# A routed first layer moved into token order, and a second stage that gathers its result

## The reference

```
xn  = layernorm(x)
# linear attention, 16 heads of 16
q, k = elu(xn@Wq+bq)+1, elu(xn@Wk+bk)+1 ; v = xn@Wv+bv
kv   = sum over the sequence of k (x) v, per head
att  = (q @ kv) / max(q . sum(k), 1e-6)  @ Wo + bo
# feed-forward: a shared expert and a routed one
swiglu(z) = silu(first half of z) * second half
shared = swiglu(xn @ w_in.T) @ w_out.T           # 256 -> 1024 -> 512 -> 256
group  = argmax(xn @ wg.T + gb)                  # 2 groups of 4 experts
p      = softmax(expert logits within the group) * group probability
h      = swiglu(xn @ w1.T)                       # the same w1 for all experts
routed = sum over the two best experts e of  p[e] * (h @ w2[e].T)
out    = x + att + shared + routed
```

## Time and profile before

| | |
|---|---|
| median of 3 runs | 1070.78 us (1067.65 to 1071.2) |
| profiled execution, own time | 1058.75 us |
| its span, first to last instruction | 1056.8 us |
| mean granted TensorE clock | 0.995 of full speed |
| busy: TensorE / weight loads | 1012.4 (96%) / 910.4 us (86%) |
| busy: VectorE / ScalarE / GpSimd | 672.9 (64%) / 398.8 (38%) / 491.5 us (47%) |
| DMA | 64.55 MB in 55585 packets, mean 61 GB/s |

### The profile page before, as it was taken

How to read it: one execution, slowest core, us unless ns; L and a number is a source line. 1 busy time by engine, 2 the same in 40 slices (tenths; PEclk the granted TensorE clock), 3 DMA queues, 4 the chain that set the end, 5 groups by cost and what they waited for, 6 DMA issues and landing times.

```text
span 1056.8 us, 21589 instructions
## 1 busy us (share of the span) xinstructions
PE 1012.4 (96%) x6662; PEld 910.4 (86%) x6663; DVE 672.9 (64%) x1681; ACT 398.8 (38%) x676; POOL 491.5 (47%) x489
## 2 busy tenths in 40 slices
PE   5999999999999999999999889999999999999996
PEld 5889879888888888898888779999999999999996
DVE  7887797788779778877977634444443444444343
ACT  3454354345445444544444322222222222222221
POOL 5343343534343443334344445555555555555534
PEclk9999999999999999999999899999999999999999
DMA  8012111201211120211111032222222122222321
GB/s 269 24 53 73 52 40 52 72 20 57 68 52 40 52 72 26 64 54 52 40 52 53 12 82 71 64 72 61 69 69 71 63 69 69 63 68 69 65 45 21
DMA packets 55585, 64.55 MB, mean 61 GB/s; under 512 B 18829, under 2 KB 45581, under 8 KB 55568
## 3 DMA queue, kind: packets, MB, share of 16 engines
q1 hardware_dynamic: 42624, 35.86, 11.3%
q0 software_dynamic: 12944, 28.47, 9.9%
HBM read 37.16 MB, written 28.58 MB: 62 GB/s over the span
## 4 chain that ended last, share of the span: by engine, by line
PE 60%; DVE 22%; issue 12%; ACT 3%; DMA 1%; POOL 1%; SPq 0%; DVEq 0%; ACTq 0%; POOLq 0%
PE bank L309 19%; PE bank L310 19%; PE bank L311 18%; DVE xn L715 4%; PE bank L381 3%; DVE stats L701 2%; DVE gated L795 1%; DVE lmax L726 1%; DVE phiq L825 1%; DVE phik L808 1%; PE bank L502 1%; ACT expt L617 1%; ACT expt L619 1%; ACT gated L598 1%; DVE rn L857 1%
## 5 line engine op out<-in xcount | busy, mean ns | idle before, releaser
L598 ACT ACTIVATE gated<-bank 128x512 f32<-128x512 f32 (+1 forms) x140 | 83.0, 593 | 264.2 <-PE bank L311 224.6
L309 PE MATMUL bank<-wexp_hi,h_hi 128*128 x600 | 170.2, 284 | 0.3 <-DVE h_lo L961 0.3
L310 PE MATMUL bank<-wexp_lo,h_hi 128*128 x600 | 168.5, 281 | 0.0
L311 PE MATMUL bank<-wexp_hi,h_lo 128*128 x600 | 168.5, 281 | 0.0
L997 POOL TENSOR_TENSOR h_lo<-gated,h_hi 128x512 fp32r<-128x512 f32 x64 | 83.8, 1309 | 170.5 <-ACT h_hi L602 169.0
L602 ACT CAST h_hi<-gated 128x512 fp32r<-128x512 f32 (+1 forms) x140 | 86.4, 617 | 159.1 <-DVE gated L795 158.4
L795 DVE TENSOR_TENSOR gated<-gated,bank 128x512 f32<-128x512 f32 (+1 forms) x140 | 95.2, 680 | 77.5 <-ACT gated L598 77.5
L971 DVE SCALAR_TENSOR_TENSOR res<-bank,cur,res 128x256 f32<-128x256 f32 x150 | 62.2, 477 | 123.1 <-PE bank L311 120.7
L1058 POOL DMA_INDIRECT out<-res,idx_cur x75 | 74.2, 989 | 102.9 <-DVE res L971 88.9
L309 PE MATMUL bank<-xnT_hi,wexp_hi 128*128 128x512 f32 (+1 forms) x304 | 117.7, 387 | 1.0 <-DVE xnT_lo L952 1.0
L310 PE MATMUL bank<-xnT_lo,wexp_hi 128*128 128x512 f32 (+1 forms) x304 | 117.7, 387 | 0.0
(11 more groups left out here) (171 smaller groups left out, 2506.6 us busy)
## 6 DMA issues: line engine op xcount, KB each, us to landing
xt<-x SPq DMA_DIRECT2D x16, 512.0 KB, 3.6
xn_d<-xn SPq DMA_DIRECT2D x16, 512.0 KB, 2.9
base_d<-res SPq DMA_DIRECT2D x16, 512.0 KB, 4.5
wstage<-w_exp SPq DMA_DIRECT2D x16, 320.0 KB, 4.2
tab_d<-wexp_hi SPq DMA_DIRECT2D x12, 128.0 KB, 5.5
phik<-tab_d SPq DMA_DIRECT2D x76, 2.0 KB
xn<-xn_d,idx_next POOLq DMA_INDIRECT x76, 2.8
res<-base_d,idx_cur POOLq DMA_INDIRECT x76
```

Source lines behind the costliest of these rows:

```text
L309: e.matmul(to, w_hi, m_hi_, start=first_, stop=False, skip_group_check=free)
L310: e.matmul(to, w_hi, m_lo_, start=False, stop=False, skip_group_check=free)
L311: return e.matmul(to, w_lo, m_hi_, start=False, stop=last_, skip_group_check=free)
L598: act.activation(gated[:, j % 2, 0:cols], bank[gate_bank][:, 0:cols], ACT.Silu).then_inc(sil, 1)
```

## The change

What moves:

- The routed first layer is computed in stage one, in token order: per tile 12 matmuls with the tile's xnT as weights and 512 columns of w1 moving (`routed(t, banks)`), a SiLU on ScalarE and a gate on VectorE into hs[t], a [128 tokens, 512] tile. hs lies in the buffers of phik and expt. w1's rows are permuted on the host in blocks of 32, and both halves of it are loaded and split before batch 0.
- GpSimd scatters, per batch and tile, the row of the table, the row of hs to `h_d` (2 KB) and the row of res to `base_d` (1 KB) to the token's place in its class: 12 indirect DMAs where there were 4. The stores of xn and of base by SyncE go; x is loaded a second time, into res, after the scatters of the batch before have landed.
- xn is made in place of x. VectorE makes ranks and table rows right after gate 1, ahead of the norm of the next batch, in every batch.
- The head sums have phiq moving and 32 columns of khead as weights, four tiles in the four column groups of bank 6; rn is [128, 128] (tile and head on the partitions), and `rdiag` puts each tile's block in its own 128 columns, so that one matmul of 512 columns per chunk spreads it. The transposes of rn go.
- After stage one SyncE writes zeros behind the end of each class in `h_d` and `base_d`: 13 times a position read and two stores.
- Stage two goes tile by tile, eight tiles per turn. SyncE loads the table piece and, in four DMAs of 32 partitions, the tile's h, 512 B per descriptor, so that VectorE's transpose of 32x32 blocks completes a transpose of 128x512. ScalarE makes the high part and issues the load of base; VectorE makes the low part and the two additions; TensorE has only the second layer, 24 matmuls of 256 columns.

The core of the diff (stage one, TensorE and VectorE):

```diff
+            def routed(t, banks):
+                for half in range(2):
+                    for c in range(DC):
+                        mm = mm3(pe, bank[banks[half]][:, :], xnT_hi[:, c, t * P:(t + 1) * P], xnT_lo[:, c, t * P:(t + 1) * P],
+                                 w1_hi[:, c, half * H1:(half + 1) * H1], w1_lo[:, c, half * H1:(half + 1) * H1], c == 0, c == DC - 1)
+                mm.then_inc(rh_done, 1)
...
-                for t in range(TB):
-                    for c in range(DC):
-                        mm = pe.matmul(bank[6][:, 16 * t:16 * t + 16], phiq[:, c, t * P:(t + 1) * P], khead[:, c, :],
+                for c in range(DC):
+                    for t in range(TB):
+                        mm = pe.matmul(bank[6][32 * t:32 * t + 32, 0:P], khead[:, c, :], phiq[:, c, t * P:(t + 1) * P],
...
+                routed(0, (0, 1))        # behind the transposes of kvm; then m, which waits for gate 2
+                hidden(3, (3, 7))
+                routed(1, (0, 1))
+                # spread; routed(2, (3, 7)); routed(3, (0, 1)); transposes(b + 1); y
...
                 gate(b, 1, 1)
+                ranks_in(b)
+                table_rows(b)
+                norm(b + 1)
                 gate(b, 2, 4)
+                dve.tensor_scalar(rn, bank[6][:, 0:P], EPS_N, None, ALU.max).then_inc(kstep, 1)
+                dve.reciprocal(rn, rn).then_inc(kstep, 1)
+                dve.tensor_copy(rhigh.bitcast(f32r), rn).then_inc(kstep, 1)
+                dve.scalar_tensor_tensor(rn, rhigh, low_row, rn, ALU.mult, ALU.add).then_inc(kstep, 1)
+                dve.tensor_tensor(rdiag, rn.unsqueeze(1).broadcast_to([P, TB, P]),
+                                  own_block.unsqueeze(2).broadcast_to([P, TB, P]), ALU.mult).then_inc(rn_rdy, 1)
+                routed_gate(b, 0, 1)
+                # m_lo, normalise(b + 1), gate 3, routed_gate 1, qn, qn_lo, routed_gate 2 and 3, t_low
```

GpSimd and SyncE in stage one:

```diff
+                pool.wait_ge(r_ld, 16 * (b + 1))
+                pool.tensor_tensor(res[:, :, :], res[:, :, :], bo..., ALU.add).then_inc(res_rdy, 1)
+                split(b + 2, b * UNIT + W1, UNIT)
+                low(0, ...); low(1, ...); reciprocal_root(b + 1)
+                for t in range(TB):
+                    scatter(tab_d, rows[:, t, :], t, row_st)
+                low(2, ...); scatter(h_d, hs[0], 0, hs_st); low(3, ...)
+                for t in range(1, TB):
+                    wait_apart(pool, rg_rdy, TB * b + t + 1)
+                    scatter(h_d, hs[t], t, hs_st)
+                for t in range(TB):
+                    wait_apart(pool, base_rdy, DC * b + t // 2 + 1)
+                    scatter(base_d, res[:, t, :], t, base_st)
...
+                    sp.wait_ge(t_done, DC * (b + 1))
+                    sp.dma_start(xt[:, :, :], x_rows(b + 1)).then_inc(x_ld, 16)
+                wait_apart(sp, base_st, 16 * TB * b)
+                sp.dma_start(res[:, :, :], x_rows(b)).then_inc(r_ld, 16)
+                sp.wait_ge(wexp_split, b + 2)
+                sp.dma_start(wstage[:, 0:UNIT], w_exp[:, bass.ds(b * UNIT + W1, UNIT)]).then_inc(w_ld, 16)
```

Stage two (SyncE, TensorE, ScalarE, VectorE):

```diff
+            def tiles_in(q):
+                wait_apart(sp, tab_ld, 16 * TB * q)
+                at = [sp.value_load(info_i[0:1, 2, bass.ds(q * TB + t, 1)], min_val=0, max_val=SENT) for t in range(TB)]
                 for t in range(TB):
+                    sp.dma_start(tab[:, bass.ds(q * TB + t, 1), :]..., tab_d[bass.ds(at[t], P), :]).then_inc(tab_ld, 16)
+                    wait_apart(sp, tr_done, TB * q + t - 3)
+                    for i in range(4):
+                        sp.dma_start(hb[t][32 * i:32 * i + 32, :].rearrange("p (b f) -> p b f", b=TB),
+                                     h_d[bass.ds(at[t], P), i * P:(i + 1) * P].rearrange("(b p) f -> p b f", b=TB)).then_inc(h_ld[t], 16)
...
+                for t in range(tiles):
+                    at = [pe.value_load(info_i[0:1, n, bass.ds(g * GT + t, 1)], ...) for n in range(2)]
+                    wait(pe, ysum, GT * g + t - 7)
+                    pe.wait_ge(tlo2, GT * g + t + 1)
+                    for n in range(2):
+                        for j in range(HC):
+                            off = at[n] + (W1 + j * D)
+                            mm = mm3(pe, bank[t][:, n * D:(n + 1) * D], rh_hi[t % TB][:, j, :], rh_lo[t % TB][:, j, :],
+                                     wexp_hi[:, bass.ds(off, D)], wexp_lo[:, bass.ds(off, D)], ...)
...
+                    act.wait_ge(tr_done, GT * g + t + 1)
+                    wait(act, sw_done, GT * g + t - 3)
+                    act.copy(rh_hi[t % TB], hT[t % 2]).then_inc(thi2, 1)
+                    at = act.value_load(info_i[0:1, 2, bass.ds(g * GT + t, 1)], min_val=0, max_val=SENT)
+                    wait_apart(act, out_st[t], 16 * g)
+                    act.dma_start(ring[t], base_d[bass.ds(at, P), :]).then_inc(b_ld[t], 16)
...
+            def transposed(t, g):
+                dve.wait_ge(h_ld[t % TB], 64 * (2 * g + t // TB + 1))
+                dve.transpose(hT[t % 2]..., hb[t % TB]...).then_inc(tr_done, 1)
...
+                    add(t, g, 0)
+                    ahead(low, t + 3, g, last)
+                    dve.wait_ge(ystep, GT * g + t + 1)
+                    add(t, g, 1)
+                    ahead(transposed, t + 4, g, last)
```

More of the change, by code:

```diff
@@ new lines, in _ @@
+            rounds(sp, load, B)
+            sp.wait_ge(zero_set, 1)
+            sp.wait_ge(ends_rdy, 1)
+            for n in range(NCLS + 1):
+                if n < NCLS:
+                    g, k = divmod(n, NCLS // 2)
+                    j, i = PAIRS[k]
+                    end = sp.value_load(ends[0:1, 16 * g + 4 * j + i:16 * g + 4 * j + i + 1], min_val=0, max_val=SENT)
+                    tail = bass.ds(end, P)
+                else:
+                    tail = slice(SENT, ROWS)
+                sp.dma_start(h_d[tail, :], zeros).then_inc(zero_st, 16)
+                sp.dma_start(base_d[tail, :], zeros[:, 0:D]).then_inc(zero_st, 16)
@@ L373, in _, with transposes @@
+            tiles_in(0)
+            with sp.Fori(1, NH) as q:
+                tiles_in(q)
         @block.tensor
         def _(pe):
-            def transposes(banks, done, free_sem, free_of, ready, ready_n):
-                pe.wait_ge(ready, ready_n)
+            def transposes(b):
+                pe.wait_ge(xn_rdy, b + 1)
                 for c in range(DC):
-                    wait(pe, free_sem[c], free_of[c])
                     for t in range(TB):
-                        mm = pe.transpose(bank[banks[c]][:, t * P:(t + 1) * P], xn[:, t, c * P:(c + 1) * P], ident)
-                    mm.then_inc(done, 1)
@@ L835, in batch @@
                 ins.then_inc(kstep, 1)
[L836 removed]
+                gate(b, 0, 7)
                 for c in range(DC):
@@ new lines, in add, with ahead @@
+            def add(t, g, n):
+                wts = cur[:, t // TB, t % TB, :].bitcast(f32)
+                dve.scalar_tensor_tensor(ring[t], bank[t][:, n * D:(n + 1) * D], wts[:, n + 1:n + 2], ring[t],
+                                         ALU.mult, ALU.add).then_inc((ystep, ysum)[n], 1)
+            def ahead(step, t, g, last):
+                if not last or t < LAST_TILES:
+                    if t < GT:
+                        step(t, g)
+                    else:
+                        step(t - GT, g + 1)
@@ new lines, in entries, with scatter @@
+                wait_apart(pool, cur_rdy, 2 * g + half + 1)
+                pool.tensor_copy(idx_cur[:, half, :], cur[:, half, :, 0]).then_inc(idxc_rdy, 1)
+            def scatter(g, half, tiles=TB):
+                wait_apart(pool, idxc_rdy, 2 * g + half + 1)
+                for t in range(TB * half, TB * half + tiles):
+                    wait_apart(pool, ysum, GT * g + t + 1)
+                    pool.indirect_dma_start(out, bass.IndirectOffsetOnAxis(ap=idx_cur[:, half, t % TB:t % TB + 1], axis=0), ring[t], None,
+                                            bounds_check=N - 1, oob_is_err=False).then_inc(out_st[t], 16)
@@ L1082, in _ @@
+            def group(g, last):
+                if last:
+                    scatter(g, 0, LAST_TILES)
+                else:
+                    entries(g, 1)
+                    scatter(g, 0)
+                    entries(g + 1, 0)
+                    scatter(g, 1)
+            entries(0, 0)
             rounds(pool, group, NG)
-            scatter(NG - 1, LAST_TILES)
-            pool.wait_ge(out_st, 16 * (TB * (NG - 1) + LAST_TILES))
+            for t in range(GT):
+                pool.wait_ge(out_st[t], 16 * (NG if t < LAST_TILES else NG - 1))
```

574 lines of the change are left out of this document (261 added, 313 removed).

## The result

The changed kernel took 1135.82 us (1133.21 to 1138.55), and the kernel before, run beside it, 1069.79: a ratio of 1.0631, 95% interval 1.0601 to 1.0661. Forecast was 1102, a ratio of 1.0295. The direction was right, the loss more than twice as large. Run again later, the same program gave 1.0248 (1.0226 to 1.0270) and 1.0264 (1.0247 to 1.0281). Most of the miss therefore lies not in the program but in something that it met in the run of the result. "The first trace" is the one of 1.0631, "the repeat" that of 1.0248.

A forecast was written before the change was run, and what follows sets the result against it. Both stages were taken as TensorE-bound before, stage two as bound by SyncE's DMA issue after. 743.6 to the last batch + 46.4 + 285 + 13 = 1088 us of span, scaled to 1102; range 1062 to 1135.

The forecast's parts named there:

- starts 0.6 apart without a pause, tiles 3.8 apart: Stage two: SyncE issues DMAs at this even spacing and sets the pace, 75 x 3.8 = 285 us.
- upper bound of 4.8 per tile: Stage two, SyncE: us per tile if each h load costs the 0.57 with half as much again.
- the extra 0.05 each: Stage two, SyncE: added to each of four h DMAs for three-dimensional patterns, bringing 3.62 to 3.8 us per tile.
- 24 matmuls of 256 columns per tile, 2.87 us: Stage two, TensorE's whole work per tile; times 75 = 215 us.
- stage two runs at SyncE's pace: Stage two: SyncE's 3.8 us per tile lies above TensorE's 2.87, so 75 tiles take 285 us.
- Rival B: Stage two: SyncE keeps up, h DMAs 0.39 apart, TensorE sets 2.9 us per tile; 1036 us, chance 0.14.
- 48.5: Stage one: period per batch in us, 46.5 of TensorE work plus waits of 2.1; bounds 45.5 and 50.5.
- lower bound of 0.4: Stage one, TensorE: head sums in us with the four column groups side by side; 1.7 was taken.
- rival C: Stage two: TensorE, idling 0.9 of every 3.8 us, drops to half clock; about 4.6 per tile, 1157 us, chance 0.08.
- (1): Stage one: GpSimd's later work holds VectorE's router operations; one-hot rows come 0.7 us after TensorE wants them.
- (2): Stage one: TensorE waits for gate 2 ahead of the m matmuls, gate 2 ending at 25.7, TensorE there at 24.3; 1.4 us.
- D (period of 52): Stage one: VectorE's added work, its queue order and GpSimd's passes make the period 52; +49 us, 1151, chance 0.10.

The follow-up runs named there:

- e5: Changed kernel with one DMA of 128 rows of 2 KB per tile for h instead of four of 32 rows: 1.0229 to the kernel before.

## Why the prediction was wrong, point by point

- **The step that failed:** "starts 0.6 apart without a pause, tiles 3.8 apart". In the run of the result SyncE's queue nearly stood still for 4 to 5 us in nearly every group of four, so a tile took 4.13. From the first DMA of stage two to the end the kernel took 332 us instead of 295.5, which is 36.5 of the 44.6 us missed; the repeat, without the pause, took 297.5. Nothing in the trace before showed it. There a burst of four scatters (707.92 to 711.79) stands beside four position loads of 262 to 277 ns. A pause would have cost nothing either: SyncE issued its table groups some 6.8 us apart and the last at 727, long before TensorE needed them. My upper bound of 4.8 per tile held the 4.13, by another cause.
- **SyncE's cost without the pause** was near: 14.0 us per group in the repeat, 3.5 per tile against 3.8. The four h loads start 0.50 apart, not 0.62; the extra 0.05 each that I took from the loads of x was not there, nor the 0.57 for the h loads.
- **TensorE was mis-sized:** "24 matmuls of 256 columns per tile, 2.87 us" left out two register loads per tile, which had been free in the kernel before. A tile takes 3.65, in the repeat 3.70 in the mean. So the two queues were nearly level, with TensorE a little behind: in the repeat SyncE's 3.5 is the shorter, and the forecast "stage two runs at SyncE's pace" holds only with the pause. Rival B, which put the pace at 2.9 once SyncE kept up, could not have happened: e5, where SyncE has time to spare, gave 1.0229. That the forecast fits the repeat (1.0295 against 1.0248) is partly luck. SyncE's term was too large and TensorE's too small; the 75 tiles took 277 us instead of 285, but 20 us more lie ahead of the first matmul (8.5) and behind the start of the last (11.7), against 13 in the forecast.
- **Stage one:** period 48.66 against 48.5, but by compensation. The head sums in column groups take 0.58 us from their start to the next kind (428.26 to 428.84), near my lower bound of 0.4, not 1.7. The wait for gate 2 is 2.44, not 1.4. From the first k matmul (408.31) gate 2 ends at 26.4 instead of 25.7, since beside GpSimd's h_lo pass one table-row instruction of VectorE (L805) takes 0.86 where the same operation at L801 takes 0.22; and TensorE is there at 24.0 instead of 24.3. With gate 2 fixed by VectorE, what the head sums save only lengthens the wait behind them. (The terms as written add to 48.6, and rival C's 0.8 us on 75 tiles to 60, not 55; neither changes the reading.) Timeline of TensorE in batch 8 of the first trace, the counterparts of the earlier trace rows:

```profile
425.09 0.23 PE L471 MATMUL bank<-oh,triones 128*128 128x128 bf16 x1 [0.79 <-DVE oh L781]
...
428.26 0.64 PE L486 MATMUL bank<-phiq,khead 128*32 128x128 f32 x16
...
434.75 1.13 PE L507 MATMUL bank<-wo,relut 128*128 128x256 f32 x4 [2.44 <-DVE gated L813]
...
447.13 0.60 PE L398 MATMUL bank<-stay,xt 128*128 128x128 f32 x4
```

  Waits (1) and (2) were the right ones, and no wait stands ahead of the transposes, as forecast. The mechanism of (1), a pass of GpSimd that catches VectorE's small operations, is visible too:

```profile
417.92 2.40 DVE L756 TENSOR_SCALAR gg<-gg 128x4 f32<-128x4 f32 x1
```
```profile
417.90 2.40 POOL L1055 TENSOR_TENSOR res<-res,bvo 128x1024 f32<-128x1024 f32 x1 [5.17 <-DMA res<-x]
```

  An operation on four columns lasts exactly as long as GpSimd's addition. In the repeat the same addition (411.71 to 414.10) catches a later instruction (L763, 2.12 us from 412.02), and TensorE does not wait for the one-hot rows: 0.9 us per batch hang on it. The forecast 48.5 therefore fits the first trace, and the repeat has 47.79.
- **Batch 0:** the second batch starts at 68.4, not 64.6. GpSimd's split of w1 holds a VectorE operation for 4.70, and TensorE waits 4.15 for the one-hot rows; I had counted the splits only against h_lo.
- **VectorE's transpose:** 0.71 us, forecast 0.7. That VectorE stays under TensorE holds too: it is busy 144.56 of 251 us in the body of the repeat, TensorE 209.24. The transposes of one stretch of the first trace:

```profile
L983 DVE STREAM_TRANSPOSE phiq<-xt x4: 711/712/712, 902.5 to 922.5; 128x512 f32<-128x512 f32 x4
```

- **Rivals:** C (clock) did not occur, 0.98 to 1.00 in the body of stage two at three quarters busy. D (period of 52) did not. The Trainium skill (DMA: Bandwidth & Descriptors, Issuing engines are not separate DMA queues) calls the sequencer's time usually small beside the DMA itself. For one h load the trace agrees: 0.50 us from start to start, 1.9 from issue to landing (median, first trace). It does not follow that the issues can be left out: with one h load per tile (e5) SyncE has time to wait for VectorE, with four (the repeat) it waits for nothing and its loop takes 14.0 us per group, register work and issues. The waits of SyncE in e5, from 900 to 1050:

```profile
SPq L277 <- DVE phiq L981: 69.9, 31, 2.5
```

## What to carry to other kernels

Count the instructions of a queue, not the work they start: here register loads 0.65 us apart and DMA starts 0.5 us apart make up SyncE's 3.5 us per tile, two register loads some 0.75 us apart bring TensorE from 2.87 to 3.65, and one of TensorE's two taken away gave about 34 us (1.0229 to 0.9914). An instruction that cost nothing under other work has to be counted anew when that work moves away. Before explaining a difference between two kernels, have both in one comparison: two "cures" here were first read against a number from another comparison. And when a wait goes, walk on to the next: gate 2 alone gave next to nothing, the whole order 44 us.

## What the runs showed that I had not expected

The same program differed by 47 us (1135.82 against 1088.45) while the kernel before differed by less than 8 (1069.79 against 1062.03): the changed kernel leans on SyncE's queue and on which VectorE operation meets GpSimd's addition, and the kernel before, whose SyncE runs far ahead, does not lean on the first. SyncE's queue fell to two or three instructions per 0.7 us for 4 to 5 us beside GpSimd's bursts of scatters in five executions, and in none of the later ones. Eight products of 32 weight columns and 128 moving ones, two in each of four column groups (16 rows in the profile), took 0.58 us together.
